# Another order for a head's sixth step, and one read of each tile's expert

## The reference

```python
x = x + xattn(ctx, layernorm(x))     # x: 4 x 1024 x 256, ctx: 4 x 154 x 256, 16 heads of 64
#   q = lat @ Wq;  k, v = split(concat([x, lat]) @ Wkv)      lat: normalised x, x: normalised ctx
#   out = softmax(q k^T / 8) v;  out @ Wout
x = x + ffn(layernorm(x))            # E = 8 experts, 256 -> 1024 -> 256
#   p = softmax(x @ Wg + bg);  e = argmax(p)
#   y = (silu(x @ W1[e] + b1[e]) @ W2[e] + b2[e]) * p[e]
```

## Time and profile before

| | us |
|---|---|
| median of 3 runs (2122.77 to 2123.02) | 2122.85 |
| the profiled execution, whole | 2125.33 |
| its span, first to last instruction | 2123.6 |
| TensorE busy in the span | 1986.5 |
| VectorE, ScalarE, GpSimd busy | 1552.3, 1515.9, 1442.5 |
| mean granted TensorE clock | 0.983 of full |

### The profile page before, as it was taken

One profiled execution on the slowest core, in us unless ns is written; L12 is line 12 of the kernel. 1 busy time (PEld: TensorE's weight loads), 2 busy tenths in 40 slices (PEclk: granted clock), 3 DMA queues, 4 the chain that ended last, 5 costly groups with the idle time before them and its releaser, 6 DMA issues. The chain is left out here.

```text
span 2123.6 us, 63298 instructions
## 1 busy us (share of the span) xinstructions
PE 1986.5 (94%) x25468; PEld 1361.5 (64%) x25468; DVE 1552.3 (73%) x2972; ACT 1515.9 (71%) x1981; POOL 1442.5 (68%) x818
## 2 busy tenths in 40 slices
PE   4999999999999999999999999999999998589997
PEld 1566666667666666676666666766666666466765
DVE  8777777776788887777788877777888874645554
ACT  3688878875887777758877777677777776155664
POOL 3588887883888878838878888567888886023332
PEclk8999999999999999999999999999999999799999
DMA  5222222222322222222222222222222221271110
GB/s 187 49 57 62 55 54 61 63 49 65 82 54 55 54 55 54 54 68 74 62 57 55 55 54 55 58 66 63 59 55 54 55 54 34 94 303 36 45 45 24
DMA packets 129586, 140.03 MB, mean 66 GB/s; under 512 B 45570, under 2 KB 94390, under 8 KB 128150
## 3 DMA queue, kind: packets, MB, share of 16 engines
q1 hardware_dynamic: 125557, 126.58, 23.2%
q0 software_dynamic: 3744, 9.39, 1.5%
HBM read 55.15 MB, written 26.15 MB: 38 GB/s over the span
## 5 line engine op out<-in xcount | busy, mean ns | idle before, releaser
L777 POOL TENSOR_TENSOR probs_split<-probs,probs_split 128x1024 f16<-128x1024 f32 x576 | 1223.2, 2136 | 281.1 <-ACT probs_split L882 272.9
L875 ACT ACTIVATE probs<-score 128x1024 f32<-128x1024 f32 (+1 forms) x640 | 655.9, 1025 | 346.4 <-PE score L1216 338.2
L1056 DVE TENSOR_REDUCE max_parts<-aux 128x1 f32<-128x512 f32 x1024 | 685.0, 689 | 92.6 <-PE aux L1216 84.3
L882 ACT ACTIVATE probs_split<-score 128x1024 f16<-128x1024 f32 (+1 forms) x640 | 653.6, 1021 | 0.0
L1326 PE MATMUL acc<-values,probs_split 128*128 128x65 f16 x5120 | 554.4, 193 | 7.6 <-POOL probs_split L777 7.4
L1330 PE MATMUL acc<-values,probs_split 128*128 128x64 f16 x4608 | 519.9, 194 | 0.0
L1331 PE MATMUL acc<-values,probs_split 128*128 128x65 f16 x4608 | 517.8, 192 | 0.0
L1326 PEld LDWEIGHTS acc<-values,probs_split 128*128 128x128 f16 x5120 | 463.7, 97 | 64.0 <-POOL probs_split L777 11.1
L1216 PE MATMUL aux<-k_high,q_both 128*128 128x512 f16 (+1 forms) x1536 | 458.5, 333 | 44.6 <-DVE values L1052 31.2
L1216 PE MATMUL score<-q_both,k_high 128*128 128x512 f16 (+1 forms) x1280 | 484.0, 378 | 2.9 <-DMA q_max<-max_row 2.5
L1216 PE MATMUL score<-q_max,k_low 65*128 65x512 f16 (+1 forms) x1280 | 486.6, 380 | 0.0
(11 more groups left out here) (179 smaller groups left out, 2244.1 us busy)
## 6 DMA issues: line engine op xcount, KB each, us to landing
k_high<-raw SPq DMA_DIRECT2D x128, 147.2 KB, 2.5
q_both<-raw SPq DMA_DIRECT2D x128, 128.0 KB, 2.5
piece_in<-in_L_ffn_W SPq DMA_DIRECT2D x64, 256.0 KB, 3.2
halves<-piece_out SPq DMA_DIRECT2D x128, 128.0 KB, 2.4
k_low<-raw SPq DMA_DIRECT2D x64, 147.2 KB, 2.4
q_max<-raw SPq DMA_DIRECT2D x64, 128.0 KB, 2.5
w<-halves SPq DMA_DIRECT2D x16, 512.0 KB
w<-halves SPq DMA_DIRECT2D x8, 1024.0 KB
```

The lines of the kernel that those rows point to most:

```text
L777: nc.gpsimd.tensor_tensor(out=low[0:r, :], in0=prob(h, j)[0:r, :], in1=high[0:r, :], op=ALU.subtract)\
L875: nc.scalar.activation(prob(h, j)[0:r, :], score[j % 2][0:r, :], ACT.Exp, scale=SCALE)\
L882: nc.scalar.activation(halves(h, j)[0][0:r, :], score[j % 2][0:r, :], ACT.Exp, scale=SCALE)\
L1056: nc.vector.tensor_reduce(max_parts[g % 2][:, t, c:c + 1], bank[:, :], AX.X, ALU.max)\
```

## The change

There are two parts. In the sixth step the four places held nothing, values, turn, first maximum; now they hold nothing, turn, first maximum, values. ScalarE takes a values chunk of the first two places between the two exponentials as before, and one of the last two places behind both. In `experts()`, TensorE reads a tile's expert once, two tiles ahead, in the middle of each step; before, the reads for tiles 0 and 1 of each group of four stood at the group's start, and the next group's tile 0 was also read within the group before.

```diff
-    ("", "v", "turn", "first"),
+    ("", "turn", "first", "v"),
...
                     if of < HEADS:
                         exponent(of, jj)
-                    for chunk in BESIDE[h][j]:
-                        if chunk and chunk[0] == "v":
-                            value_high(chunk)
+                    early, late = [[c for c in BESIDE[h][j][at:at + 2] if c and c[0] == "v"] for at in (0, 2)]
+                    for chunk in early:
+                        value_high(chunk)
                     if of < HEADS:
                         high_half(of, jj)
+
+                    for chunk in late:
+                        value_high(chunk)
...
-            e = expert_of(0, 0)
+
+            experts_of = {0: expert_of(0, 0)}
             for c in range(KF):
-                upward(0, 0, e, c)
-
-            experts_of = {}
+                upward(0, 0, experts_of[0], c)
+            experts_of[1] = expert_of(0, 1)
 
             def step(i, u):
 
                 more = exists(i, u + 1)
-                if u == 0:
-                    experts_of[0], experts_of[1] = expert_of(i, 0), expert_of(i, 1)
+                k = number(i, u)
                 for c in range(KF):
                     if more:
-                        upward(i, u + 1, experts_of[u + 1], c)
-                    downward(i, u, experts_of[u], c)
+                        upward(i, u + 1, experts_of[k + 1], c)
+                    downward(i, u, experts_of[k], c)
                     if c == BANK:
                         turn(i, u + 2)
-                        if u + 2 <= OWN and exists(i, u + 2):
-                            experts_of[u + 2] = expert_of(i, u + 2)
+                        if exists(i, u + 2):
+                            experts_of[k + 2] = expert_of(i, u + 2)
```

## The result

The changed kernel takes **2098.75 us** (median of 4 runs, 2098.46 to 2099.94), the kernel before 2122.82 us beside it. The ratio is 0.9888, with a 95% interval of 0.987 to 0.9905: 24.1 us, or 1.1%, less. Forecast were 2093 us and a range of 2080 to 2104.

The account below looks back on a forecast made before the run. TensorE, busy 94% of the span, was taken to bound the kernel. Step order 24.5 us (40 + 3.1 - 13.6 - 3.4 - 1.2 - 0.4) plus experts 5.2 gave 29.7 off 2122.85: 2093 us, range 2080 to 2104.

Parts of the forecast that it names:

- the stall: Sixth step: TensorE's wait at the first maximum for the values' bank goes, 40 us gained over 62 heads.
- The copies: Sixth step: the first maximum, now earlier, waits for SP's copies of keys and queries in 28 heads, 13.6 us lost.
- rival (a): At the first maximum the copies are never late, so 13.6 us come back: 2080 us; chance 20%, half of it included.
- The values: Sixth step: the values, now last, start 1.09 us after the scores are through; no wait at their start was counted.
- z: In the 12 heads with a z chunk, z waits for the values' bank: 3.4 us lost.
- ScalarE's normalising: In six heads it stands ahead of the exponential and delays the values: 1.2 us lost.
- the tie: Seventh step, second half: a maximum wants the values' bank about when it frees, 0.03 us in hand; 0.4 us charged.
- The send to `q_max`: Attention: the send starts almost 2 us earlier, so four waits of a score on it go, 3.1 us gained.
- The experts' reads: Experts' stage: TensorE reads `tile_expert` 39 times instead of 49, net 5.2 us gained.
- (b) to (d): Attention: copies late in every head, 2131 us, 3%; GpSimd or ScalarE sets the pace, 2118, 5%; slower signals, 2103, 14%.

Follow-up runs that it names:

- order_only: The changed kernel with the expert reads of before in `experts()`, so only the new sixth step: 2103.96 us, ratio 0.9900 to the kernel before.
- norm_step3: The changed kernel with VectorE's gate-row normalisation moved from the end of a head's fifth step to its fourth, the reciprocal a step earlier: 2092.41 us, ratio 0.9846.
- norm2: The changed kernel with gate rows normalised on ScalarE in the third step, shifts by two small ScalarE instructions, reciprocal two steps earlier: 2091.54 us, ratio 0.9838.
- experts_only: The changed kernel with the sixth step's old order, so only the new expert reads: 2119.53 us, ratio 0.9974 to the kernel before.

## Why the prediction was right, and where not

**The bound and the stall.** Forecast 40 us gone, measured 40.5. The reading that nothing but TensorE sets the pace held, also for kernels up to 26 us faster than the changed one.

**The copies.** Forecast 13.6 us, measured 11.7 in the profiled execution and 13.5 in `order_only`. All 24 waiting heads are among the 28 named. To take the spread of landings from the trace of before was right because the late heads belong to the program: rival (a), another execution free of them, would have needed another program. With no cause known this was in part luck. The Trainium skill's page "DMA: Bandwidth & Descriptors", section "Anatomy of one DMA", has about 2.0 us as a DMA's fixed cost; the section is on DMAs that GpSimd issues, and these are SP's. The figure fits the median of 2.0 us from issue to landing, and not the 3.5 of heads with an instruction packet; by it alone the term would have been near zero.

**The values.** Here a step failed. "From V they start at 0.51 + 0.22 + 0.37 = 1.09" takes for granted that their bank is free. It is the turn's bank, and I had checked only that VectorE's *values* no longer stand ahead of the turn's copy, not what else does. In 24 heads a normalisation stands there. Its 1.69 us were in the trace of before, covered. This cost 8.5 us, which are gone in `norm_step3` and `norm2`. It is twice the 4.3 us by which this part of the forecast fell short (24.5 against 20.2). That the whole came so close is luck: other terms, each named here, made up for half of it.

**z, ScalarE's normalising, the tie.** Forecast 3.4, 1.2 and 0.4 us; measured 2.9 and 1.1 for the last two together. These small terms were sized nearly rightly.

**The send to `q_max`.** Forecast 3.1 us gone, measured 1.8: heads 15 and 37 still wait, up to 0.7 us. They are two of the four that waited before. In each an instruction packet starts 1.2 to 1.3 us after the send, and in the four of before one starts within 1 us of it, on either side. Head 37 is also a gated one, whose copy the normalisation delays. But in other heads a packet as near to the send made no wait (26, 33 and 41 now, nine before), so this cause is not shown.

**What was not in the sum.** The ninth step's first maximum cost 1.0 us more, small gaps 2.2 us less, and the attention stage started 0.9 us earlier.

**The experts' reads.** Forecast 5.2 us; measured 5.3 in `experts_only`, with an interval of 3.4 to 7.6, and 6.2 in the experts' stage between the two profiles. From tile 7's step on, where the forecast counted, the kernels with the old reads (before, `order_only`) take 201.5 and 200.6 us and those with the new (the changed kernel, `experts_only`) 195.5 and 194.9, which is 5.1 to 6.5 less; the seven tiles ahead vary between 47.6 and 52.4 us whatever the reads. (The forecast's "eight full groups from tile 8" are seven and one of three tiles; its eight fourth tiles come out with tile 7's.) The estimate from the Trainium skill's same page was 6.0. The runs don't tell it from 5.2.

**The sum.** 5.6 us lie between 2093 and 2098.75. About 3.3 are terms: 26.4 us between the profiles against 29.7 (4.3 too much in the step order, 1.0 too little in the experts). The other 2.3 are the basis. I took the terms from a profiled execution 2.5 us above its median and subtracted them from the median. Rivals (b) to (d) did not come: the copies are late in 24 heads, not in all; no other engine took over; the waits that slower signals would have made, at z and behind the values, are as forecast or smaller.

## What to carry to other kernels

When a wait is removed or a place moved forward, list for the new first user of each buffer every instruction ahead of the one that frees it, with its duration in that place: a long one that nobody waited for is still long. Two waits in a row hide each other, so mending one alone pays less than its size (here 3.6 of 11.4 us came back at the next). Where lateness can't be removed, put work that doesn't need the late thing in front of the work that does: here that took a few lines and gave 4 us more than removing both causes did.

## What the runs showed of the hardware

- **VectorE is held by GpSimd.** A normalisation of 128x256 from SBUF to SBUF takes 0.41 us with GpSimd idle, 1.69 with 1.54 us of a GpSimd instruction left, 0.64 with 0.49 left, always ending 0.15 us after it (24 of 24 each). One of 128x8 with two SBUF sources takes 1.52 with 1.49 left. The subtraction of a head's last tile (L1134 after, 32x1024, two SBUF sources) takes 1.22 us alone and 2.42 with 1.34 left. Reductions and casts from PSUM beside the same GpSimd instruction keep their 0.69 us. The Trainium skill, page "SBUF — State Buffer", section "Who interferes with whom", describes this: VectorE and GpSimd share a pair of ports as an exclusive lock, held for the whole instruction, which some forms of `tensor_scalar` take, and a VectorE instruction with two SBUF inputs contends with a GpSimd one that reads SBUF. The traces agree with it, in which instructions are held and in that a small one waits as long as a large one. The ports themselves no run here shows.
- **TensorE's instructions come through the same DMA engines as the data.** 210 packets of 16 KB, one per 256 instructions, 0.9 to 1.4 us each for the most part (1.74 at most); a small copy that meets one lands 0.9 to 1.6 us later, and SP's issue can take up to 1.99 us instead of 0.6. Which heads are hit follows the count of TensorE's instructions, so that 128 more of them move the lateness to other heads. That it is the packet that blocks, and on which engine, I infer; no view shows a copy's packet queued behind it.
- **An increment of a semaphore takes 0.15 us** on TensorE's queue when nothing stands between.
